# A quarter of each group's convolution as four accumulating products on TensorE, the recurrence's scan in two halves

## What is computed

```python
xn = layernorm(x)
# branch 1, the mixer
x_proj, z = split(xn @ W_in.T)                  # 256 channels each
xc = causal_depthwise_conv(x_proj, conv_w)      # 4 taps along the sequence
x_conv = silu(xc + conv_b)
dt = softplus((x_conv @ W_x[2*S:].T) @ W_dt.T + b_dt)
alpha = clip(sigmoid(dt * 0.1), 0.01, 0.99)
gated = (1 - alpha) * sigmoid(mean(x_conv @ W_x[:S].T)) * x_conv
h = linear_recurrence(alpha, gated)             # h[t] = alpha[t] h[t-1] + gated[t]
y = (h * sigmoid(mean(x_conv @ W_x[S:2*S].T)) + D * x_conv) * silu(z)
mixer = y @ W_out.T
# branch 2, the experts: 2 of 8 for each token
ffn = sum over the 2 of  p_e * (silu(xn @ w1[e]) * (xn @ w3[e])) @ w2[e]
out = x + mixer + ffn
```

## Time and profile before

| | |
|---|---|
| median of three executions | 519.69 us (518.01 to 522.01) |
| the profiled execution | 520.43 us |
| its span, first to last instruction | 518.6 us |
| instructions in the span | 8,083 |
| mean granted TensorE clock | 0.947 |

### The profile page before, as it was taken

How to read it: one execution, slowest core, us unless ns; L and a number is a source line. 1 busy time by engine, 2 the same in 40 slices (tenths; PEclk the granted TensorE clock), 3 DMA queues, 4 the chain that set the end, 5 groups by cost and what they waited for, 6 DMA issues and landing times.

```text
span 518.6 us, 8083 instructions
## 1 busy us (share of the span) xinstructions
PE 435.6 (84%) x2070; PEld 303.0 (58%) x2070; DVE 429.6 (83%) x896; ACT 321.3 (62%) x419; POOL 320.5 (62%) x306
## 2 busy tenths in 40 slices
PE   0888577888898888888899999999999878988863
PEld 0767223434444444434689888898888777544343
DVE  5999996899999999996797676776777654699995
ACT  2885375778888888889444444444444422679870
POOL 1027777887888887780067777777777777632210
PEclk9999686889999999999799999999999989989887
DMA  9501119311111111114355666666666663099997
GB/s 249 149 18 53 54 49 196 67 41 44 42 42 42 37 42 42 32 43 109 84 145 171 188 190 182 189 174 180 184 184 184 184 183 103 2 162 164 227 228 192
DMA packets 71258, 62.87 MB, mean 121 GB/s; under 512 B 9098, under 2 KB 63534, under 8 KB 71232
## 3 DMA queue, kind: packets, MB, share of 16 engines
q1 hardware_dynamic: 60224, 37.08, 27.5%
q0 software_dynamic: 11008, 25.52, 18.9%
HBM read 39.08 MB, written 24.53 MB: 123 GB/s over the span
## 4 chain that ended last, share of the span: by engine, by line
PE 37%; DVE 36%; issue 16%; ACT 5%; SPq 4%; DMA 2%; DVEq 0%; ACTq 0%
PE PD L710 11%; DVE acc L1133 6%; DVE ybuf L1098 3%; DVE ybuf L1104 3%; PE PA L676 3%; PE PD L659 3%; PE PA L672 3%; PE PA L673 3%; PE PB L672 3%; PE PB L676 3%; PE PB L673 3%; PE PA L591 2%; PE PC L579 2%; DVE gbuf L983 2%; DVE gbuf L1078 2%
## 5 line engine op out<-in xcount | busy, mean ns | idle before, releaser
L467 POOL DMA_INDIRECT moe_in<-xn,slot_u x128 | 158.1, 1235 | 72.7 <-issue 41.6
L475 POOL DMA_INDIRECT moe_out<-xnT,dst_u x144 | 146.3, 1016 | 71.5 <-issue 40.0
L1133 DVE SCALAR_TENSOR_TENSOR acc<-PA,cw,acc 128x510 f32<-128x510 f32 (+2 forms) x96 | 68.7, 735 | 10.5 <-ACT acc L861 10.3
L1293 DVE TENSOR_TENSOR xn<-xn,PB 128x1024 f32<-128x1024 f32 x36 | 43.9, 1220 | 36.6 <-PE PB L676 33.0
L710 PE MATMUL PD<-xn 128*128 128x128 f32 x576 | 71.4, 278 | 0.9 <-DVE xnT L1349 0.9
L710 PEld LDWEIGHTS PD<-xn 128*128 128x128 f32 x576 | 68.2, 194 | 1.0 <-issue 1.0
L579 PE MATMUL PC<-xc,Wc 128*128 128x512 f32 x128 | 61.1, 622 | 2.6 <-ACT xc L902 2.6
L591 PE MATMUL PA<-xnT,WinT 128*128 (+1 forms) x64 | 38.3, 728 | 29.4 <-DVE acc L1133 28.4
L933 ACT ACTIVATE xn<-PA 128x1024 f32<-128x1024 f32 x36 | 36.9, 1026 | 35.9 <-PE PA L676 32.6
L552 PE MATMUL PD<-xc,WgB 128*128 128x512 f32 x128 | 57.5, 592 | 0.0
L915 ACT ACTIVATE whi<-xn 128x512 fp32r<-128x512 f32 x36 | 22.7, 632 | 37.6 <-DMA xn<-in_L_ffn_w_dram 37.6
(11 more groups left out here) (190 smaller groups left out, 905.1 us busy)
## 6 DMA issues: line engine op xcount, KB each, us to landing
xn<-in_L_ffn_w_dram SPq DMA_DIRECT2D x120, 128.0 KB, 2.4
xn<-moe_in SPq DMA_DIRECT2D x32, 266.0 KB, 3.5
xacc<-moe_out POOLq DMA_DIRECT2D x16, 512.0 KB, 7.9
out_dram<-xacc SPq DMA_DIRECT2D x7, 512.0 KB, 9.3
moe_out<-xnT,dst_u POOLq DMA_INDIRECT x144
moe_in<-zrow SPq DMA_DIRECT2D x8, 266.0 KB, 6.0
moe_in<-xn,slot_u POOLq DMA_INDIRECT x128, 2.4
xn<-moe_in SPq DMA_DIRECT2D x8, 133.0 KB, 2.6
```

Source lines behind the costliest of these rows:

```text
L467: gp.indirect_dma_start(xs_dram, bass.IndirectOffsetOnAxis(ap=slot_u[:, k, j:j + 1], axis=0), xn_row[:, j, :], None).then_inc(s_scat, 16)
L475: gp.indirect_dma_start(yt_dram, bass.IndirectOffsetOnAxis(ap=dst_u[:, t, j:j + 1], axis=0), yo[t % OUTS][:, j, :], None, bounds_check=PAI ...
L1133: ins = ve.scalar_tensor_tensor(a_v, p_v[:, :, 0:SEQ - j], cw[:, c_, TAPS - 1 - j:TAPS - j], a_v, ALU.mult, ALU.add)
L1293: ve.tensor_tensor(hid[b], sil, PB[:, :], ALU.mult).then_inc(s_hid, 1)
```

## The change

The first half's (channels 0 to 127) convolution for the first sequence of each group, one quarter of the group's 1,024 columns, is done by TensorE. Setup makes four weight matrices: row d of W_in's first 128 rows scaled by conv_w[d, k], for each tap k (four tensor_scalar on GpSimd into a view of sz, once all weights are loaded), transposed by TensorE into PB in the third round and copied by ScalarE into a new tensor Wtap. In a turn, four products accumulate in PA[:, 0:256]: tap offset j over the first 256 - j columns of the input, written to columns j to 255. The other three quarters are projected as before, as one product of 256 columns and one of 512.

ScalarE applies Silu with the bias straight from PA to that quarter of xc (new semaphore s_xq), then writes the base of acc for the remaining 256 columns of half 0 and for half 1; its final Silu covers 768 columns. Ahead of the early Silu it waits for the slot of xc to be free (s_ch). TensorE waits for s_xq in addition to s_taps before the next projection. VectorE's taps of half 0 cover the second sequence only, those of half 1 both.

The scan becomes two instructions, one for each half; the step is signalled by the second. ybuf is gone, its values stand in hbuf, and a scratch view of the routing moves from xc to y2.

```diff
--- before.py
+++ after.py
@@ -108,7 +108,7 @@
         al = sb("al", [P, HALVES, GROUP])
         gbuf = sb("gbuf", [P, HALVES, GROUP])
         hbuf = sb("hbuf", [P, HALVES, GROUP])
-        ybuf = sb("ybuf", [P, HALVES, GROUP])
+        Wtap = sb("Wtap", [P, TAPS, P])
         y2 = sb("y2", [P, HALVES, GROUP])
         thg = sb("thg", [P, SLOT3, 2, GROUP])
 
@@ -141,6 +141,7 @@
         wx_raw = flat(ebuf[:, :, :])[:, 0:512].rearrange("p (a b) -> p a b", a=2)
         wxB = ebuf[0:STATE, 1, 0:256]
         wxC = ebuf[0:STATE, 1, 256:512]
+        tap_raw = sz[:, 0, 0, :].rearrange("p (k d) -> p k d", k=TAPS)
         wo_raw = flat(th[:, :, :])[:, 0:256]
         wdtT = flat(th[:, :, :])[:, 512:1024].rearrange("p (a b) -> p a b", a=2)
         inv16 = th[0:STATE, 0, 256:256 + P]
@@ -187,7 +188,7 @@
         den = gbuf[:, 1, 384:448]
         cmp_m = flat(xc[:, 2, :, :])[:, 0:EXPERTS * STEPS_T].rearrange("p (e m) -> p e m", e=EXPERTS)
         cmp_t = flat(xc[:, 2, :, :])[:, 256:256 + ENTRIES * BINS].rearrange("p (t e) -> p t e", e=BINS)
-        cmp_s = flat(xc[:, 1, :, :])[:, 0:ENTRIES * BINS].rearrange("p (t e) -> p t e", e=BINS)
+        cmp_s = flat(y2[:, :, :])[:, 0:ENTRIES * BINS].rearrange("p (t e) -> p t e", e=BINS)
         tail = flat(xc[:, 2, :, :])[:, 896:896 + ENTRIES]
         at_t = flat(xc[:, 2, :, :])[:, 936:936 + ENTRIES]
         odd = flat(xc[:, 2, :, :])[:, 976:976 + ENTRIES]
@@ -202,6 +203,7 @@
         s_zrow = sem("s_zrow")
         s_fill = sem("s_fill")
         s_cst = sem("s_cst")
+        s_tapw = sem("s_tapw")
         s_wtp = sem("s_wtp")
         s_wcp = sem("s_wcp")
         s_dve = sem("s_dve")
@@ -230,6 +232,7 @@
         s_taps = sem("s_taps")
         s_cv = sem("s_cv")
         s_xc = sem("s_xc")
+        s_xq = sem("s_xq")
         s_sz = sem("s_sz")
         s_u = sem("s_u")
         s_g = sem("s_g")
@@ -457,6 +460,10 @@
             gp.affine_select(out=tri, in_=tri, compare_op=ALU.is_ge, fill=1.0,
                              base=0, pattern=[[-1, P]], channel_multiplier=1).then_inc(s_cst, 1)
 
+            gp.wait_ge(s_wld, 16 * 10)
+            for k in range(TAPS):
+                gp.tensor_scalar(tap_raw[:, k, :], win_raw[:, 0, :], cw[:, 0, k:k + 1], None, ALU.mult).then_inc(s_tapw, 1)
+
             for n, (q0, qn) in enumerate(CHUNKS):
                 gp.wait_ge(s_slot, n + 1)
                 gp.wait_ge(s_xn, rows_v(q0 + qn))
@@ -514,6 +521,9 @@
                         for kb in range(2):
                             last = pe.matmul(PB[:, ib * 256:(ib + 1) * 256], wx_raw[:, kb, ib * P:(ib + 1) * P],
                                              wdtT[:, kb, :], start=(kb == 0), stop=(kb == 1))
+                    pe.wait_ge(s_tapw, TAPS)
+                    for k in range(TAPS):
+                        last = pe.transpose(PB[:, 512 + k * P:512 + (k + 1) * P], tap_raw[:, k, :], ident[:, :])
                 last.then_inc(s_wtp, 1)
 
             pe.wait_ge(s_cst, 14)
@@ -583,13 +593,18 @@
             def mix(g, slot, a, b, c, d):
                 static = isinstance(g, int)
                 if a:
-                    src = xnT[:, bass.ds(g * GROUP + GROUP, GROUP)] if not static else \
-                        xnT[:, (g + 1) * GROUP:(g + 2) * GROUP]
+                    def columns(at, n):
+                        return xnT[:, bass.ds(g * GROUP + (GROUP + at), n)] if not static else \
+                            xnT[:, (g + 1) * GROUP + at:(g + 1) * GROUP + at + n]
+                    src = columns(0, GROUP)
                     if not (static and g + 1 < 1):
                         pe.wait_ge(s_taps, g + 1)
-                    for c_ in range(HALVES):
-                        last = pe.matmul(PA[:, c_ * GROUP:(c_ + 1) * GROUP], WinT[:, c_ * P:(c_ + 1) * P], src,
-                                         start=True, stop=True)
+                        pe.wait_ge(s_xq, g + 1)
+                    for j in range(TAPS):
+                        pe.matmul(PA[:, j:SEQ], Wtap[:, TAPS - 1 - j, :], columns(0, SEQ - j),
+                                  start=(j == 0), stop=(j == TAPS - 1))
+                    pe.matmul(PA[:, SEQ:GROUP], WinT[:, 0:P], columns(SEQ, SEQ), start=True, stop=True)
+                    last = pe.matmul(PA[:, GROUP:2 * GROUP], WinT[:, P:2 * P], src, start=True, stop=True)
                     last.then_inc(s_xp, 1)
                 if d:
                     out(g, slot, b)
@@ -642,7 +657,7 @@
             for g in range(12, GROUPS):
                 rows(g)
             pe.wait_ge(s_xnT, GROUPS)
-            pe.wait_ge(s_wcp, 8)
+            pe.wait_ge(s_wcp, 9)
             mixer(pe, mix, -1, 0)
             ranks(2)
 
@@ -779,6 +794,8 @@
                                    ACT.Copy).then_inc(s_wcp, 1)
                 else:
                     act.activation(Wc[:, :, :], PB[:, 0:512].rearrange("p (a b) -> p a b", a=2),
+                                   ACT.Copy).then_inc(s_wcp, 1)
+                    act.activation(Wtap[:, :, :], PB[:, 512:1024].rearrange("p (a b) -> p a b", a=TAPS),
                                    ACT.Copy).then_inc(s_wcp, 1)
                     act.activation(dsk8[:, :], dsk[:, :], ACT.Copy, scale=-8.0).then_inc(s_wcp, 1)
                     act.activation(nbdt[:, :], bdt[:, :], ACT.Copy, scale=-1.0).then_inc(s_wcp, 1)
@@ -857,10 +874,13 @@
                     act.wait_ge(s_xp, g + 2)
                     if not (static and g + 1 < 1):
                         act.wait_ge(s_xc, g + 1)
-                    for c_ in range(HALVES):
-                        last = act.activation(acc[:, c_, :], PA[:, c_ * GROUP:(c_ + 1) * GROUP], ACT.Identity,
-                                              bias=cb[:, c_:c_ + 1], scale=cw[:, c_, TAPS - 1:TAPS])
-                    last.then_inc(s_tap0, 1)
+                    if not (static and g < 2):
+                        act.wait_ge(s_ch, g * CHAIN - CHAIN)
+                    act.activation(xc[:, nxt, 0, 0:SEQ], PA[:, 0:SEQ], ACT.Silu, bias=cb[:, 0:1]).then_inc(s_xq, 1)
+                    act.activation(acc[:, 0, SEQ:GROUP], PA[:, SEQ:GROUP], ACT.Identity,
+                                   bias=cb[:, 0:1], scale=cw[:, 0, TAPS - 1:TAPS])
+                    act.activation(acc[:, 1, :], PA[:, GROUP:2 * GROUP], ACT.Identity,
+                                   bias=cb[:, 1:2], scale=cw[:, 1, TAPS - 1:TAPS]).then_inc(s_tap0, 1)
                 if c:
 
                     act.wait_ge(s_dt, g)
@@ -899,7 +919,7 @@
                                    scale=0.5).then_inc(s_thg, 1)
                 if a:
                     act.wait_ge(s_taps, g + 2)
-                    act.activation(xc[:, nxt], acc[:, :, :], ACT.Silu).then_inc(s_xc, 1)
+                    act.activation(xc[:, nxt].rearrange("p a b -> p (a b)")[:, SEQ:2 * GROUP], flat(acc[:, :, :])[:, SEQ:2 * GROUP], ACT.Silu).then_inc(s_xc, 1)
 
             mixer(act, mix, -1, 0)
             softmax_exp(2)
@@ -1089,29 +1109,29 @@
                 elif part == 2:
                     after(4)
 
-                    step(ve.tensor_tensor_scan(hbuf[:, :, :].rearrange("p a b -> p (a b)"),
-                                               al[:, :, :].rearrange("p a b -> p (a b)"),
-                                               gbuf[:, :, :].rearrange("p a b -> p (a b)"), 0.0, ALU.mult, ALU.add))
+                    for c_ in range(HALVES):
+                        last = ve.tensor_tensor_scan(hbuf[:, c_, :], al[:, c_, :], gbuf[:, c_, :], 0.0, ALU.mult, ALU.add)
+                    step(last)
                 elif part == 3:
                     after(5)
 
-                    step(ve.scalar_tensor_tensor(ybuf[:, :, :], gates[:, 1:2, :].broadcast_to([P, HALVES, GROUP]), 1.0,
+                    step(ve.scalar_tensor_tensor(hbuf[:, :, :], gates[:, 1:2, :].broadcast_to([P, HALVES, GROUP]), 1.0,
                                                  hbuf[:, :, :], ALU.add, ALU.mult))
                 else:
                     after(6)
 
                     for c_ in range(HALVES):
-                        last = ve.scalar_tensor_tensor(ybuf[:, c_, :], xc[:, prv, c_, :], dsk8[:, c_:c_ + 1],
-                                                       ybuf[:, c_, :], ALU.mult, ALU.add)
+                        last = ve.scalar_tensor_tensor(hbuf[:, c_, :], xc[:, prv, c_, :], dsk8[:, c_:c_ + 1],
+                                                       hbuf[:, c_, :], ALU.mult, ALU.add)
                     step(last)
                     after(7)
                     ve.wait_ge(s_out, g)
                     if part == 4:
-                        ve.tensor_tensor(y2[:, :, :], ybuf[:, :, :], sz[:, prv], ALU.mult).then_inc(s_y2, 1)
+                        ve.tensor_tensor(y2[:, :, :], hbuf[:, :, :], sz[:, prv], ALU.mult).then_inc(s_y2, 1)
                     else:
                         for h in range(2):
                             at = slice(h * SEQ, (h + 1) * SEQ)
```

(7 more changed lines are left out.)

## The result

| | before | after |
|---|---|---|
| median of 20 runs each | 520.50 us (517.03 to 523.70) | 522.54 us (521.69 to 525.38) |
| profiled execution, its span | 520.43, 518.6 | 522.72, 520.9 |
| granted TensorE clock, mean of the span | 0.947 | 0.967 |
| steady turn of the mixer | 14.62 | 15.28 |
| first expert transpose | 245.26 | 249.11 |

The ratio is 1.0045 with a 95% interval of 1.0027 to 1.0064. The changed kernel is slower by about half a per cent, not by the 1.5% that I forecast: 527.6 was predicted, 522.5 measured, inside the range of 520.5 to 533. In the sense of the chances it is no change within 1%, which had 0.20, not slower, which had 0.70. Rival 2's sum, 521.2, is nearer to the measured time than the forecast's.

The account below looks back on a forecast made before the run. The mixer was taken to set the experts' start, its turn becoming bound by the wait for the base of acc. Experts 6.5 us later plus 1.4 after them gave +7.9: 527.6 us beside the 519.69 median, range 520.5 to 533.

Parts of the forecast that it names:

- Rival 2: TensorE's extra columns keep the full clock in turns 1, 2 and the last project: -6.4 us, so 521.2; chance 0.14.
- The way round: From VectorE's last tap over TensorE and ScalarE to its next first tap: grows from 3.66 to 5.23 us.
- drain: In TensorE's projection: some 0.27 us taken off the 1.98 us before pricing 762 more columns, giving 1.27 us.
- The wait: VectorE idle about 1.4 us before each steady turn's first tap, for ScalarE's base of acc; turn 15.32 us.
- Rival 1: VectorE's saving counts: experts start 3.8 us earlier, capped by their input load, last turns give 1.4; 514.5 us; chance 0.10.
- The scan: VectorE's scan split into two halves: +0.08 us a turn; by the rule on pieces, the split can only cost.
- Turns 1 to 4: First mixer turns, partly at low clock: start differences of -1.58, +0.23, +1.14 and +1.08 us up to turns 1 to 4.
- Turn 11: Last mixer turn before the experts: TensorE's output product waits for the projection, +0.55 us up to the gate tanh.
- The experts: Expert stage: VectorE has room there for the split scan, so 0 us change.
- After the experts: Mixer turns 12 to 14 and the tail: +1.4 us, with running sums of +0.76 after turn 12, +1.00 after turn 13.
- Rival 3: Longer TensorE idle drops the clock in up to 7 steady turns: +7 us, so 534.6; chance 0.11.

Follow-up runs that it names:

- experiment 1: Kernel before with its first 512-column projection product done twice between last tap and base: 541.57 us, ratio 1.0399.
- experiment 4: Changed kernel with VectorE's taps of half 0 at full width again, the quarter's result computed but unused: 546.14 us, ratio 1.0493.
- experiment 6: Changed kernel with the quarter's products after the others, into PB, and base before Silu: 512.48 us; with one tap also moved earlier, 507.91 us.
- order3: Changed kernel with the quarter's products last, into PB, base before Silu, and a half 0 tap ahead of the output product's add: 507.91 us, ratio 0.9779.
- experiment 5: Changed kernel with the scan whole again, one instruction of 1,024 columns: 522.46 us, ratio 1.0055.
- experiment 3: Changed kernel run once more, nothing edited, for a second trace: 522.78 us, ratio 1.0071.
- experiment 2: Kernel before with 768 more columns of product in the z projection, which nobody waits for: 517.05 us, ratio 0.9949.

## Why the prediction was right and wrong

- **The way round.** Predicted 5.23 us, measured 5.18. In it the projection was put at 1.98 + 1.30 = 3.28 and took 3.26; ScalarE's three instructions were put at 1.61 and took 162.59 - 160.99 = 1.60. The price by columns, from the setup's row, was right. The 0.27 us taken off as drain stand in no row of before; experiment 1 bears them out, since six instructions take 2.84 us and four 1.98, so one is 0.43 and 1.98 - 4 x 0.43 = 0.26 is left.
- **The wait.** Predicted 1.4 us, measured 1.27 to 1.38. The turn: predicted 15.32, measured 15.28. Experiments 1, 4 and 6 confirm the cause from three sides: work put on the way costs (15.41 at full clock, 17.03 with the drop), VectorE work put back costs in full (16.04), the same work taken off the way costs nothing (14.14).
- **Rival 1**, that the saving counts, failed as argued. Its cap had a flaw of its own. I let the experts start at most 3.8 us earlier, since the load was due at 241.5; in order3 they start 8.9 us earlier, which they can because the load is itself issued 6.75 us earlier.
- **The scan.** The turn's price was right, 0.08 predicted and 0.07 measured. The step that failed is "the split can only cost": I weighed the instruction by itself, and quoted the rule on pieces, without looking at who shares an interface with it. In the changed kernel nothing came of the error, as experiment 5 shows: the earlier load wasn't used. In a faster one it was 11 us.
- **Turns 1 to 4.** The step that failed is "Turn 2: 3.67 becomes about 5.0". I multiplied each stretch of low clock by the work in it, as if the clock were a property of the place. The projection of turn 2 took 3.26 us at full clock in the first trace and 4.96 in the second. Turn 1 was put at 1.81 more than before and took 1.70 more in the first trace, 0.66 in the second; turn 2 was put at 0.91 more and took 0.91 less in the first, 0.79 more in the second. Together they were 32.08 us before and 32.87 and 33.53 in the two traces of after, where I had reckoned 34.80. Turn 3, predicted at 3.28 for its projection, ran at full clock as I had put it. Of the gap of 2.2 us in the table 1.9 are these two turns, and 0.2 stood before them. What decides in one execution whether turn 2 runs low, no run shows.
- **Turn 11** was put at +0.55 and came out at +0.42.
- **The experts.** "0" was predicted for them, and this failed too: 2.2 us were won. 1.0 us is the clock in the first tile, by the windows of experiment 3, and no gain of the change to rely on, since one kernel gave 6.43 and 4.88 there. Another 0.4 us is the second tile, whose first transposes took 1.05 us in before and 0.60 in after. From the third tile to the thirty-first the two keep step. The last 0.75 us come in the five tiles behind, where TensorE waits for the loads of expert inputs; in the second trace of after nothing is won there (all of its 3.0 us are in the first two tiles), so this is no gain to rely on either.
- **After the experts.** Predicted +1.4, measured +0.7. Turn 12 gave +0.68 of the forecast 0.76; turn 13 gave -0.17 instead of +0.24. Its projection was put down from 2.50 to 3.28 rightly (3.27), and its way round grew from 4.07 to 5.01, by the 0.95 forecast. The step that failed is the -0.71 from first to last tap, which held before's turn 13 for a steady one. It took 11.18 us there, not 10.80, with VectorE waiting 0.26 us for an output product that ran low (3.07 us long); in after it took 10.06. So the difference was -1.12.
- **Rival 2** had 0.14, and its sum, 521.2, came nearer to 522.5 than the forecast's 527.6, in part by luck. It took away 6.4 us for turns 1 and 2 and the last project. Turns 1 and 2 gave 1.9; the last project stayed at 5.40 in one trace and fell to 3.70 in another; and what the experts and turn 13 gave stands in no term of it. The busier kernel of experiment 2 prices the effect at 2.7 us, without any other change. The forecast's 7.9 less 2.7 would have been 5.2, or 524.9, still 2.4 above the median, of which 0.7 is behind the experts and 0.75 in the last five tiles.
- **Rival 3** didn't occur in the changed kernel, whose granted clock was 1.00 in the steady turns. It lay close: with 1.6 to 1.7 us of idle time the clock held in every steady turn, with 2.1 to 2.2 us in one kernel it fell in every turn from 3 to 10, with 2.4 to 2.5 us in another in five of these eight.

The sum was wrong in one direction, and more than half of the 5.6 us has one reason: it held unfavourable rows of a single execution fixed (low clock in turns 1 and 2, in the first two tiles) and added to them. That is 1.9 + 1.4 us, and part of the 0.4 in turn 13 is of the same kind. The Trainium skill (TensorE: Matmul & The Clock Gate, What's actually happening) names activity as what releases the lower clock; experiment 2, in which more work goes with a higher granted clock (0.951 to 0.967), agrees with it, and the prediction gave that rule 0.14 on an argument that no row carried. That the changed kernel's 0.967 has the same cause is likely and not shown, since no run separates the two.

## What to carry to other kernels

Moving work from the busiest engine to another gains only if the work doesn't land between that engine's last instruction of one turn and its first of the next; draw that way round, add up both sides, and put the new work behind what the busy engine waits for (here 522.5 became 507.9 us). Price low clock as a chance, not as a property of a turn: more work off the way can give some of it back, and a longer wait on the way can bring on a drop larger than the work itself. When a VectorE instruction is split or merged, look at GpSimd's queue as well, and at who waits for that.
